# MLP stage written out: signals, split engines, gate and add apart

## The chip, the cores and the metric

One core of one Trainium2 chip runs the program. The metric is the device time of one execution in microseconds (us). The kernel before took 4002.65 us, the median of three runs (3992.6 to 4006.91).

TensorE (PE) multiplies, VectorE (DVE), ScalarE (ACT) and GpSimd (POOL) work on elements, and SyncE (SP) issues the DMAs of the stage in question. Each works through its own queue in order and waits for others by semaphores.

## The reference

Two transformer blocks on x of 2 x 2048 x 512, in float32: a cross attention, then self attention, cross attention and an MLP. The change is in the MLP alone:

```python
h = layer_norm(x)
h = h * (1.0 + scale_mlp) + shift_mlp
h = jax.nn.gelu(h @ mlp_w1 + mlp_b1) @ mlp_w2 + mlp_b2
x = x + h * gate_mlp
return x
```

w1 is 512 x 2048, w2 is 2048 x 512. The modulated layer norm is written by the stage before, transposed, as `u`.

## The kernel before

`build` calls the stages one after the other; `mlp` is the last. Every float32 matrix is held as two parts of type float32r, an upper one (rounded) and a lower one (the rest), and a product is three matmuls (`PARTS`): upper by upper, upper by lower, lower by upper.

The 4096 tokens are worked through in eight chunks of 512 (W), numbered n = 2i + b: `Fori` loops on every engine run i over four steps, with b = 0 and 1 written out in the body. The hidden dimension of 2048 is 16 tiles m of 128.

PE: `hidden(m)` makes 12 matmuls from w1 and `us` into PSUM tile `ph` (L2220); `output(m)` makes 12 from `gs` and w2 into the four row tiles of `py` (L2235), which collect over m. The order is hidden 0, hidden 1, output 0, hidden 2, output 1 and so on to output 15, then hidden 0 of the next chunk.

ScalarE: GELU with bias b1 from `ph` into `gelu` (L2262). VectorE: the split of `gelu` into the upper part by a cast (L2277) and the lower by a subtraction (L2279), both into `gs`. `gelu` and `gs` have two buffers each. After output 15 VectorE gates `py` (L2283, into `gated`) and adds to `x` (L2285), four row tiles in turn, and only then comes to the splits of the next chunk. GpSimd adds the gated bias row to x as soon as x has been loaded (L2300).

The weights come in eight pieces of 1 MB, w1 and w2 in turn; hidden tiles 0 to 3 need piece 0, output tiles 0 to 3 piece 1, hidden 4 to 7 piece 2 and so on. Pieces 0 and 1 are rounded by ScalarE (L2253, L2255) and subtracted by VectorE (L2269); both first wait for `small_in`, that is b1 and four rows, or, VectorE, for ScalarE. Pieces 2 to 7 are split by GpSimd (L2291, L2293), after which it multiplies the bias row by the gate (L2295).

SP's order is: piece 0, both parts of `us` for chunk 0, piece 1, b1 (L2166), rows (L2168, L2169), pieces 2 to 7; then for each chunk the load of x (after the store of the chunk before), the load of `us` for the next chunk, and the store of x (L2189).

Of the kernel before, what the change touches and what calls it, by code (L numbers as in the profile page):

```python
# [7 lines left out]
F32 = mybir.dt.float32  # L8
# [5 lines left out]
P = 128  # L14
# [6 lines left out]
W = 512  # L21
# [16 lines left out]
def column(ap):  # L38

    return ap.rearrange("(t p) -> p t", p=P)  # L40
# [12 lines left out]
def chunk_after(i, b):  # L53
    return (i, 1) if b == 0 else (i + 1, 0)
# [2067 lines left out]
def mlp(nc, d, u_in, x_in, gate, out):  # L2122


    with nc.cleanup_on_exit(), ExitStack() as ctx:
# [12 lines left out]
        gated = sb("gated", [P, 2, W])  # L2138
# [4 lines left out]
        small_in = sem("small_in")  # L2143
        w_hi, w_lo, rows_done = sem("w_hi"), sem("w_lo"), sem("rows_done")
        late_hi, late_lo = sem("late_hi"), sem("late_lo")
# [3 lines left out]
        passed = sem("passed")  # L2149
# [8 lines left out]
        SMALL = 1 + 2 * B  # L2158

        @block.sync  # L2160
        def _(sp):
            sp.sem_inc(stored, DMA)

            def load_small():
                with nc.allow_non_contiguous_dma(reason="a short vector, once"):
                    sp.dma_start(b1[:], column(d["L1_xcond_mlp_b1"])).then_inc(small_in, DMA)  # L2166
# [4 lines left out]
            def load_u(i, b, first=False):  # L2171
                if not first:

                    sp.wait_ge(used, (2 * i + b - 1) * HT + 2)
                    sp.sem_inc(passed, 1)
                for part in range(2):
                    sp.dma_start(us[:, b, part].bitcast(F32), u_in[part, b, :, bass.ds(i * W, W)].rearrange("(t p) w -> p t w", p=P)).then_inc(u_loaded[b], DMA)  # L2177

            def chunk(i, b, left):
                sp.wait_ge(stored, DMA * (2 * i + b + 1))  # L2180


                sp.sem_inc(passed, 1)
                sp.dma_start(x[:], x_in[b, bass.ds(i * W, W), :].rearrange("(t p) c -> p t c", p=P)).then_inc(x_loaded, DMA)
                if left > 1:
                    load_u(*chunk_after(i, b))
                sp.wait_ge(x_ready, (2 * i + b + 1) * TT)
                sp.sem_inc(passed, 1)
                sp.dma_start(out[b, bass.ds(i * W, W), :].rearrange("(t p) c -> p t c", p=P), x[:]).then_inc(stored, DMA)  # L2189

            def load_weights(k):
                sp.dma_start(pieces[k][2], pieces[k][3]).then_inc(raw_in[k], DMA)  # L2192

            load_weights(0)
# [5 lines left out]
            with sp.Fori(0, CHUNKS - 1) as i:  # L2200
                for b in range(B):
                    chunk(i, b, 3)
            for b in range(B):
                chunk(CHUNKS - 1, b, B - b)
            sp.wait_ge(stored, DMA * (B * CHUNKS + 1))

        @block.tensor
        def _(pe):
            def hidden(i, b, m):
                n = 2 * i + b  # L2210
                if m == 0:
                    pe.wait_ge(w_lo, 1)
                elif m % KT == 0:
                    pe.wait_ge(late_lo, 2 * (m // KT) - 1)
                if m == 0:
                    pe.wait_ge(u_loaded[b], 2 * DMA * (i + 1))
                pe.wait_ge(gelu_done, n * HT + m + 1)
                for t in range(KT):
                    for s, (pm, pw) in enumerate(PARTS):
                        mm = pe.matmul(ph[:, m % 4], w1[pw][:, t, m * P:(m + 1) * P], us[:, b, pm, t],  # L2220
                                       start=(t == 0 and s == 0), stop=(t == KT - 1 and s == 2))
                mm.then_inc(hidden_done, 1)

            def output(i, b, m):
                n = 2 * i + b
                if m == 0:
                    pe.wait_ge(w_lo, 2)
                elif m % KT == 0:
                    pe.wait_ge(late_lo, 2 * (m // KT))
                if m == 0:  # L2230
                    pe.wait_ge(y_read, n * TT + 1)
# [7 lines left out]
            pe.sem_inc(used, 2)  # L2239
            with pe.Fori(0, CHUNKS) as i:  # L2240
                for b in range(B):
                    for m in range(HT + 1):
                        if m < HT:
                            hidden(i, b, m)
                        if m > 0:
                            output(i, b, m - 1)

        @block.scalar
        def _(act):
            act.sem_inc(gelu_done, 4)  # L2250
            act.wait_ge(small_in, DMA * SMALL)
            act.wait_ge(raw_in[0], DMA)
            act.activation(pieces[0][0], pieces[0][2], ACT.Copy).then_inc(w_hi, 1)  # L2253
            act.wait_ge(raw_in[1], DMA)
            act.activation(pieces[1][0], pieces[1][2], ACT.Copy).then_inc(w_hi, 1)  # L2255
            with act.Fori(0, CHUNKS) as i:
                for b in range(B):
                    n = 2 * i + b
                    for m in range(HT):
                        act.wait_ge(used, n * HT + m + 1)  # L2260
                        act.wait_ge(hidden_done, n * HT + m + 1)
                        act.activation(gelu[:, m % 2], ph[:, m % 4], ACT.Gelu_apprx_tanh, bias=b1[:, m:m + 1]).then_inc(gelu_done, 1)  # L2262

        @block.vector
        def _(dve):
            dve.sem_inc(y_read, 1)
            for k, (hi, lo, raw, _) in enumerate(pieces[:2]):
                dve.wait_ge(w_hi, k + 1)
                dve.tensor_tensor(lo, raw, hi.bitcast(F32), ALU.subtract).then_inc(w_lo, 1)  # L2269
            dve.wait_ge(small_in, DMA * SMALL)  # L2270
            with dve.Fori(0, CHUNKS) as i:
                for b in range(B):
                    n = 2 * i + b
                    for m in range(HT):
                        dve.wait_ge(gelu_done, n * HT + m + 5)
                        dve.wait_ge(used, n * HT + m + 1)
                        dve.tensor_copy(gs[:, m % 2, 0], gelu[:, m % 2]).then_inc(g_hi, 1)  # L2277
                        dve.wait_ge(g_hi, n * HT + m + 1)
                        dve.tensor_tensor(gs[:, m % 2, 1], gelu[:, m % 2], gs[:, m % 2, 0].bitcast(F32), ALU.subtract).then_inc(g_lo, 1)  # L2279
                    dve.wait_ge(used, (n + 1) * HT + 2)  # L2280
                    dve.wait_ge(biased, n + 1)
                    for tt in range(TT):
                        dve.tensor_tensor(gated[:, tt % 2], py[:, tt], grow[:, b], ALU.mult).then_inc(y_read, 1)  # L2283
                        dve.wait_ge(y_read, n * TT + tt + 2)
                        dve.tensor_tensor(x[:, tt], x[:, tt], gated[:, tt % 2], ALU.add).then_inc(x_ready, 1)  # L2285

        @block.gpsimd
        def _(pool):
            for k, (hi, lo, raw, _) in enumerate(pieces[2:]):
                pool.wait_ge(raw_in[2 + k], DMA)  # L2290
                pool.tensor_copy(hi, raw).then_inc(late_hi, 1)  # L2291
                pool.wait_ge(late_hi, k + 1)
                pool.tensor_tensor(lo, raw, hi.bitcast(F32), ALU.subtract).then_inc(late_lo, 1)  # L2293
            pool.wait_ge(small_in, DMA * SMALL)
            pool.tensor_tensor(brow[:], brow[:], grow[:], ALU.mult).then_inc(rows_done, 1)  # L2295
            pool.wait_ge(rows_done, 1)
            with pool.Fori(0, CHUNKS) as i:
                for b in range(B):
                    pool.wait_ge(x_loaded, DMA * (2 * i + b + 1))
                    pool.tensor_tensor(x[:], x[:], brow[:, b].unsqueeze(1).to_broadcast([P, TT, C]), ALU.add).then_inc(biased, 1)  # L2300
# [58 lines left out]
```

## Time and profile before

| what | value |
|---|---|
| median of three runs | 4002.65 us |
| profiled execution | 4006.39 us |
| its span | 4004.6 us |
| mean granted clock of PE | 0.938 |
| PE matmuls busy | 3667.1 us (92%) |
| VectorE, ScalarE, GpSimd busy | 2261.2, 1862.3, 2175.1 us |
| MLP stage in the span | 3248.20 to 4004.6 us |

The profile's times are microseconds from the start of the span. [...] "Idle before" is what an engine waited ahead of an instruction, with the one that released it. Time behind SPq is that of issuing a DMA, and landing is counted from the issue.

### The profile page before, as it was taken

Reading aid. Unit: us, or ns where it says so; the run is one execution under the profiler, and the core shown is the slowest. Engines: PE = TensorE matmul, PEld = TensorE weight load, DVE = VectorE, ACT = ScalarE, POOL = GpSimd, SP = SyncE. Lnnn points to the kernel's source line nnn. Section 1 sums busy time; section 2 is a strip of 40 time slices with the busy share of each in tenths; the row PEclk is TensorE's granted clock in tenths of the full one; section 3 lists DMA queues with packets and bytes.
Section 4 is the critical chain, followed back from the end, with each engine's and each line's share of the span. In section 5 each row is a group of like instructions: output and inputs, shape, how many; then the busy total and the mean of one; then the engine's idle time right before and its main releaser. Section 6 shows DMA issues by size and latency. Waiting matters only on the chain. (4 is left out here: it accounts for less than half of the span.)

```text
span 4004.6 us, 50633 instructions
## 1 busy us (share of the span) xinstructions
PE 3667.1 (92%) x18828; PEld 2414.8 (60%) x18828; DVE 2261.2 (56%) x3958; ACT 1862.3 (47%) x3439; POOL 2175.1 (54%) x1075
## 2 busy tenths in 40 slices
PE   4799969979999999999999999958999959999998
PEld 2577748855555445454545455427777737888887
DVE  2466642228777777777777777515665634222222
ACT  1465651113666666666666666644665521111111
POOL 0356630004888888888888888864777542000000
PEclk8798889987999999999999999978999879999999
DMA  7566556764464645556464644444576551111110
GB/s 230 146 160 168 166 159 218 222 185 105 98 143 103 149 108 127 124 110 137 101 145 106 153 101 111 120 123 111 153 179 172 134 200 42 42 42 42 42 42 31
DMA packets 231940, 505.60 MB, mean 126 GB/s; under 512 B 38151, under 2 KB 55047, under 8 KB 211751
## 3 DMA queue, kind: packets, MB, share of 16 engines
q1 hardware_dynamic: 213287, 368.49, 33.6%
q0 software_dynamic: 18432, 134.23, 15.4%
q8 instruction: 131, 2.15, 0.2%
q14 instruction: 90, 0.74, 0.1%
HBM read 215.54 MB, written 144.51 MB: 90 GB/s over the span
## 5 line engine op out<-in xcount | busy, mean ns | idle before, releaser
L2003 DVE TENSOR_REDUCE a_peak<-a_sm 128x1 f32<-128x512 f32 x2048 | 1263.3, 680 | 396.0 <-PE a_sm L1822 394.7
L1959 ACT ACTIVATE a_e<-a_st 128x512 f32<-128x512 f32 x2048 | 1061.6, 604 | 539.1 <-PE a_st L1844 506.5
L2070 POOL TENSOR_TENSOR a_esum<-a_esum,a_e 128x2048 f32<-128x2048 f32 x256 | 1210.2, 4727 | 18.8 <-POOL a_esum L2070 0.4
L1822 PE MATMUL a_sm<-a_k,a_q 96*128 96x512 f32 x2048 | 883.9, 439 | 27.9 <-DMA a_k<-s_k 27.9
L1844 PE MATMUL a_st<-a_q,a_k 128*128 128x512 f32 x2048 | 827.2, 406 | 17.4 <-ACT a_e L1959 17.2
L1822 PEld LDWEIGHTS a_sm<-a_k,a_q 96*128 96x128 f32 x2048 | 394.8, 193 | 475.8 <-DVE a_peak L2003 337.5
L1857 PE MATMUL a_acc<-a_e,a_v 128*32 128x512 f32 x4096 | 505.7, 600 | 0.0
L1844 PEld LDWEIGHTS a_st<-a_q,a_k 128*128 128x128 f32 x2048 | 387.9, 190 | 137.3 <-ACT a_e L1959 62.8
L2220 PE MATMUL mlp_ph<-mlp_us,mlp_w_hi 128*128 128x512 f32 x1024 | 336.4, 391 | 33.0 <-DVE mlp_raw_lo L2269 33.0
L2262 ACT ACTIVATE mlp_gelu<-mlp_ph,mlp_b 128x512 f32<-128x512 f32 x128 | 88.1, 688 | 595.1 <-PE mlp_ph L2220 595.1
L2277 DVE CAST mlp_gs<-mlp_gelu 128x512 fp32r<-128x512 f32 x128 | 90.8, 709 | 459.0 <-ACT mlp_gelu L2262 459.0
L2300 POOL TENSOR_TENSOR mlp_x<-mlp_x,mlp_brow 128x2048 f32<-128x2048 f32 x8 | 36.9, 4616 | 569.7 <-DMA mlp_x<-s_x 569.4
L2235 PE MATMUL mlp_py<-mlp_w_hi,mlp_gs 128*128 128x512 f32 x1024 | 317.6, 391 | 16.9 <-DVE mlp_gs L2279 16.9
L1433 POOL TENSOR_TENSOR p_e<-p_e,p_inv 128x308 f32<-128x308 f32 x256 | 173.2, 708 | 175.5 <-DVE p_inv L1109 175.4
L2220 PEld LDWEIGHTS mlp_ph<-mlp_us,mlp_w_hi 128*128 128x128 f32 x1024 | 193.5, 189 | 73.7 <-issue 33.4
L1857 PEld LDWEIGHTS a_acc<-a_e,a_v 128*32 128x32 f32 x4096 | 100.4, 108 | 219.6 <-ACT a_e L1959 124.7
L2235 PEld LDWEIGHTS mlp_py<-mlp_w_hi,mlp_gs 128*128 128x128 f32 x1024 | 191.8, 188 | 61.3 <-issue 16.3
L589 PE MATMUL p_sm<-p_ks,p_qs 96*128 96x78 f32 x1024 | 171.5, 310 | 51.0 <-DMA p_qs<-s_q 30.1
L589 PEld LDWEIGHTS p_sm<-p_ks,p_qs 96*128 96x128 f32 x1024 | 157.1, 222 | 82.8 <-DMA p_qs<-s_q 28.3
L2220 PE MATMUL mlp_ph<-mlp_us,mlp_raw_lo 128*128 128x512 f32 x512 | 200.1, 391 | 0.0
L2235 PE MATMUL mlp_py<-mlp_raw_lo,mlp_gs 128*128 128x512 f32 x512 | 199.9, 390 | 0.0
L1094 DVE TENSOR_REDUCE p_top<-p_sm 128x4 f32<-128x308 f32 x256 | 118.4, 465 | 142.5 <-PE p_sm L589 140.5
(155 smaller groups left out, 5255.1 us busy)
## 6 DMA issues: line engine op xcount, KB each, us to landing
a_esum_moved<-a_e POOLq DMA_DIRECT2D x128, 1024.0 KB, 7.3
p_qs<-s_q SPq DMA_DIRECT2D x192, 256.0 KB, 5.7
s_q<-p_qo SPq DMA_DIRECT2D x64, 512.0 KB, 7.2
a_q<-s_q SPq DMA_DIRECT2D x96, 256.0 KB, 6.8
a_k<-s_k SPq DMA_DIRECT2D x24, 1024.0 KB, 15.7
s_x<-p_x SPq DMA_DIRECT2D x16, 1024.0 KB, 4.4
s_u<-p_ut_hi SPq DMA_DIRECT2D x64, 256.0 KB, 5.8
s_u<-p_ut_lo SPq DMA_DIRECT2D x64, 256.0 KB, 6.3
```

What stands on the lines that cost most here:

```text
L589: mm = pe.matmul(sm[:, unit % 2, h * KE:(h + 1) * KE], qs[0:3 * DH, g % 2, h, qt * P:(qt + 1) * P], ks[0:3 * DH, b, g * GH + h], start=Tru ...
L1094: dve.tensor_reduce(top[:, unit % 4], src, AX.X, ALU.max).then_inc(top_done, 1)
L1433: pool.tensor_tensor(e[:, number % 2, qt, :, 0:S], e[:, number % 2, qt, :, 0:S], inv[:, number % 2, qt].unsqueeze(2).to_broadcast([P, GH, ...
L1822: mm = pe.matmul(sm[:, bank_of_unit(j, u), x * KE:(x + 1) * KE], q[0:3 * DH, j % QR, h, qt * P:(qt + 1) * P], k[0:3 * DH, g % 2, h, kc * K ...
L1844: pe.matmul(st[0:KR, place(kt, h) % RING], k[:, g % 2, h, kt * P:kt * P + KR], q[:, j % QR, h], start=True, stop=True).then_inc(score_done, 1)
L1857: mm = pe.matmul(acc[rows, 0], v[0:KR, g % 2, kt, rows], e[0:KR, (j * NKT + kt) % ER, h], start=(kt == 0), stop=(kt == NKT - 1), tile_posi ...
L1959: act.activation(e[0:KR, (j * NKT + kt) % ER, h], st[0:KR, place(kt, h) % RING], ACT.Exp, scale=SCALE).then_inc(score_read, 1)
L2003: dve.tensor_reduce(dst, src, AX.X, ALU.max).then_inc(unit_read, 1)
L2070: pool.tensor_tensor(esum[:], e[:, slot(0)] if x == 1 else esum[:], e[:, slot(x)], ALU.add).then_inc(e_added, 1)
L2220: mm = pe.matmul(ph[:, m % 4], w1[pw][:, t, m * P:(m + 1) * P], us[:, b, pm, t], start=(t == 0 and s == 0), stop=(t == KT - 1 and s == 2))
L2235: mm = pe.matmul(py[:, tt], gs[:, m % 2, pw, tt * P:(tt + 1) * P], w2[pm][:, m], start=(m == 0 and s == 0), stop=(m == HT - 1 and s == 2))
L2277: dve.tensor_copy(gs[:, m % 2, 0], gelu[:, m % 2]).then_inc(g_hi, 1)
```

## The change

The loops are gone: all engines run over n = 0 to 7 in straight code, and the semaphore counts start at zero, with the early waits left out instead of counted up in advance.

Loads: b1 has a signal of its own (`b1_in`) and is issued behind `us` and ahead of piece 1; the four rows are issued behind all weights, then `us` of chunk 1. Within a later chunk SP's order is load of x, load of the next `us`, store of x; the store waits for adds that now come in the next chunk. The last chunk is stored in four row tiles.

ScalarE loads the table for GELU ahead of all, waits for piece 0 without the small vectors, rounds pieces 0 and 1, and rounds 2 to 7 behind the GELUs of tiles 0, 1, 4, 5, 8 and 9 of chunk 0. VectorE subtracts behind the splits of the same tiles. GpSimd has the bias row and x left.

VectorE gates the four row tiles at the end of a chunk (into four buffers instead of two) and adds them to x behind the splits of tiles 0 to 3 of the next chunk; in the last chunk gate and add stay together. PE waits for each row tile of `py` by itself.

```diff
-        gated = sb("gated", [P, 2, W])
+        gated = sb("gated", [P, TT, W])
...
+        SMALL = 2 * B
+        N = B * CHUNKS
+        place = lambda n: (n // B, n % B)
+        BEHIND = {0: 2, 1: 3, 4: 4, 5: 5, 8: 6, 9: 7}
...
+            def load_u(n):
+                i, b = place(n)
+                if n >= 2:
+                    sp.wait_ge(used, (n - 1) * HT)
...
+            def load_x(n):
+                i, b = place(n)
+                if n:
+                    sp.wait_ge(stored, DMA * n)
...
+            def store_x(n):
+                i, b = place(n)
+                sp.wait_ge(x_ready, (n + 1) * TT)
...
+            def store_row(n, tt):
+                i, b = place(n)
+                sp.wait_ge(x_ready, n * TT + tt + 1)
+                sp.dma_start(out[b, i * W + tt * P:i * W + (tt + 1) * P, :], x[:, tt]).then_inc(stored, DMA)
...
             load_weights(0)
-            load_u(0, 0, True)
-            load_weights(1)
-            load_small()
-            for k in range(2, NP):
+            load_u(0)
+            with nc.allow_non_contiguous_dma(reason="a short vector, once"):
+                sp.dma_start(b1[:], column(d["L1_xcond_mlp_b1"])).then_inc(b1_in, DMA)
+            for k in range(1, NP):
                 load_weights(k)
...
+            load_rows()
+            load_u(1)
+            for n in range(N):
+                load_x(n)
+                if n and n + 1 < N:
+                    load_u(n + 1)
+                if n < N - 1:
+                    store_x(n)
+            for tt in range(TT):
+                store_row(N - 1, tt)
...
+            def output(n, m):
+                if m % KT == 0:
+                    pe.wait_ge(w_lo, 2 * (m // KT) + 2)
                 pe.wait_ge(g_lo, n * HT + m + 1)
                 for tt in range(TT):
+                    if m == 0 and n:
+                        pe.wait_ge(y_read, (n - 1) * TT + tt + 1)
...
+            act.preload_act_table_set("gelu_apprx_tanh_and_others")
+            round_weights(0)
+            round_weights(1)
+            act.wait_ge(b1_in, DMA)
+            for n in range(N):
+                for m in range(HT):
+                    act.wait_ge(hidden_done, n * HT + m + 1)
+                    if n * HT + m >= 2:
+                        act.wait_ge(g_lo, n * HT + m - 1)
+                    act.activation(gelu[:, m % 2], ph[:, m % 4], ACT.Gelu_apprx_tanh, bias=b1[:, m:m + 1]).then_inc(gelu_done, 1)
+                    if n == 0 and m in BEHIND:
+                        round_weights(BEHIND[m])
...
+            weights_rest(0)
+            weights_rest(1)
+            for n in range(N):
+                for m in range(HT):
+                    split(n, m)
+                    if n == 0 and m in BEHIND:
+                        weights_rest(BEHIND[m])
+                    if n and m < TT:
+                        add_output(n - 1, m)
+                if n == 0:
+                    dve.wait_ge(small_in, DMA * SMALL)
+                for tt in range(TT):
+                    gate_output(n, tt)
+                    if n == N - 1:
+                        add_output(n, tt)
...
-            for k, (hi, lo, raw, _) in enumerate(pieces[2:]):
-                pool.wait_ge(raw_in[2 + k], DMA)
-                pool.tensor_copy(hi, raw).then_inc(late_hi, 1)
-                pool.wait_ge(late_hi, k + 1)
-                pool.tensor_tensor(lo, raw, hi.bitcast(F32), ALU.subtract).then_inc(late_lo, 1)
```

## Rows read from the trace of the kernel before

**Rows 1.** Page: busy us of the engines, share of the span, instructions.

```profile
PE 3667.1 (92%) x18828; PEld 2414.8 (60%) x18828; DVE 2261.2 (56%) x3958; ACT 1862.3 (47%) x3439; POOL 2175.1 (54%) x1075
```

**Rows 2.** Windows, one chunk each: busy us (count) by engine, PE's clock, DMA share, GB/s.

```profile
3273.05:3373.99 100.94, 92.51 (x384) 74.55 (x385) 56.43 (x33) 12.29 (x17) 50.05 (x14) 0.96 0.19 71
3373.99:3462.55 88.56, 87.35 (x386) 72.04 (x385) 24.67 (x40) 11.01 (x16) 4.60 (x1) 1.00 0.14 48
3462.55:3551.07 88.52, 87.26 (x386) 71.95 (x385) 24.59 (x40) 12.29 (x17) 4.60 (x1) 1.00 0.13 47
```

**Rows 3.** Chain of waits, first chunk: start us, us, what.

```profile
3273.05 5.31 PE mlp_ph L2220 x12
...
3283.87 4.58 PE mlp_py L2235 x12
...
3291.19 2.72 PE mlp_py L2235 x12
```

**Rows 4.** Timeline of the head: start us, us, engine, instruction [idle before <-releaser]; then chain.

```profile
3268.57 1.91 ACT L2253 ACTIVATE mlp_w_hi<-mlp_raw 128x2048 fp32r<-128x2048 f32 x1 [27.04 <-DMA mlp_grow<-s_gates]
3273.05 0.79 PE L2220 MATMUL mlp_ph<-mlp_us,mlp_w_hi 128*128 128x512 f32 x1 [33.01 <-DVE mlp_raw_lo L2269]
...
3270.51 2.30 DVE mlp_raw_lo L2269
```

**Rows 5.** SP's issues; landings of piece 0, of both `us` parts, of piece 1.

```profile
3249.73 0.82 SPq L2192 DMA_DIRECT2D mlp_raw<-in_L_xcond_mlp_w  x1
3252.80 8.87 SPq L2168 DMA_DIRECT2D mlp_brow<-in_L_xcond_mlp_b  x1
...
DMA to landing us min/median/max: 5.6/5.6/5.6
DMA to landing us min/median/max: 7.9/9.0/10.0
DMA to landing us min/median/max: 12.4/12.4/12.4
```

**Rows 6.** Window of the first tile (columns as in rows 2); PE's waits, 3284 to 3373.

```profile
3273.00:3277.60 4.60, 4.54 (x11) 3.58 (x12) 3.70 (x1) 0.00 (x0) 4.52 (x2) 0.50 1.05 388
...
PE mlp_py L2235 <- DVE mlp_gs L2279: 8.4, 5, 2.8
```

**Rows 7.** DMA, 3260 to 3262.5, packets; then a window of 2 us.

```profile
DMA packets 2227, 0.31 MB, mean 124 GB/s; under 512 B 2080, under 2 KB 2080, under 8 KB 2227
...
3260.00:3262.00 2.00, 0.00 (x0) 0.00 (x0) 0.00 (x0) 0.00 (x0) 0.00 (x0) 0.50 0.94 139
```

**Rows 8.** Timeline: casts beside GpSimd in chunks 0 and 1, and a subtraction undisturbed.

```profile
3297.33 4.93 POOL L2293 TENSOR_TENSOR mlp_raw_lo<-mlp_raw,mlp_w_hi 128x2048 fp32r<-128x2048 f32 x1
3297.72 4.82 DVE L2277 CAST mlp_gs<-mlp_gelu 128x512 fp32r<-128x512 f32 x1
...
3331.91 0.69 DVE L2279 TENSOR_TENSOR mlp_gs<-mlp_gelu,mlp_gs 128x512 fp32r<-128x512 f32 x1
...
3392.85 2.11 DVE L2277 CAST mlp_gs<-mlp_gelu 128x512 fp32r<-128x512 f32 x1 [4.29 <-ACT mlp_gelu L2262]
```

**Rows 9.** Timeline of the first boundary, chunk 0 to chunk 1.

```profile
3374.19 0.69 DVE L2283 TENSOR_TENSOR mlp_gated<-mlp_py,mlp_grow 128x512 f32<-128x512 f32 x1 [3.50 <-PE mlp_py L2235]
3376.97 0.69 ACT L2262 ACTIVATE mlp_gelu<-mlp_ph,mlp_b 128x512 f32<-128x512 f32 x1 [7.47 <-PE mlp_ph L2220]
3379.51 0.42 DVE L2277 CAST mlp_gs<-mlp_gelu 128x512 fp32r<-128x512 f32 x1
3380.80 0.70 PE L2235 MATMUL mlp_py<-mlp_w_hi,mlp_gs 128*128 128x512 f32 x2 [1.21 <-DVE mlp_gs L2279]
```

**Rows 10.** DMA issues: count, KB each, median us to landing, of the two stages.

```profile
out<-mlp_x SPq DMA_DIRECT2D x7, 1024.0 KB, 4.3
...
s_u<-p_ut_lo SPq DMA_DIRECT2D x2, 256.0 KB, 3.2
```

**Rows 11.** DMA queue 8, 3325 to 3462: packets, MB, share of 16 engines.

```profile
q8 instruction: 5, 0.08, 0.2%
```

More of the change, by code:

```diff
@@ L2157, in mlp, with load_rows @@
         raw_in = [sem(f"raw_in{k}") for k in range(NP)]
-        SMALL = 1 + 2 * B
+        SMALL = 2 * B
+        N = B * CHUNKS
+        place = lambda n: (n // B, n % B)
+        BEHIND = {0: 2, 1: 3, 4: 4, 5: 5, 8: 6, 9: 7}
         @block.sync
         def _(sp):
[L2162 to L2166, printed above, removed]
+            def load_rows():
                 for b in range(B):
@@ L2179, in chunk @@
[L2179 to L2189, printed above, removed]
+                    sp.dma_start(us[:, n % 2, part].bitcast(F32), u_in[part, b, :, i * W:(i + 1) * W].rearrange("(t p) w -> p t w", p=P)).then_inc(u_loaded[n % 2], DMA)
@@ L2207, in _, with hidden @@
+            for tt in range(TT):
+                store_row(N - 1, tt)
+            sp.wait_ge(stored, DMA * (N - 1 + TT))
         @block.tensor
         def _(pe):
-            def hidden(i, b, m):
-                n = 2 * i + b
+            def hidden(n, m):
+                if m % KT == 0:
+                    pe.wait_ge(w_lo, 2 * (m // KT) + 1)
                 if m == 0:
[L2212 to L2217, printed above, removed]
+                    pe.wait_ge(u_loaded[n % 2], 2 * DMA * (n // 2 + 1))
+                if n * HT + m >= 4:
+                    pe.wait_ge(gelu_done, n * HT + m - 3)
@@ L2237, in output @@
                 mm.then_inc(used, 1)
[L2239 to L2246, printed above, removed]
+            for n in range(N):
+                for m in range(HT + 1):
+                    if m < HT:
+                        hidden(n, m)
+                    if m > 0:
+                        output(n, m - 1)
@@ L2248, in _, with round_weights @@
         @block.scalar
         def _(act):
[L2250 to L2262, printed above, removed]
+            def round_weights(k):
+                act.wait_ge(raw_in[k], DMA)
+                act.activation(pieces[k][0], pieces[k][2], ACT.Copy).then_inc(w_hi, 1)
@@ L2264, in _, with weights_rest @@
         @block.vector
         def _(dve):
-            dve.sem_inc(y_read, 1)
-            for k, (hi, lo, raw, _) in enumerate(pieces[:2]):
+            def weights_rest(k):
+                hi, lo, raw, _ = pieces[k]
                 dve.wait_ge(w_hi, k + 1)
                 dve.tensor_tensor(lo, raw, hi.bitcast(F32), ALU.subtract).then_inc(w_lo, 1)
[L2270 to L2285, printed above, removed]
@@ new lines, in split, with gate_output @@
+            def split(n, m):
+                dve.wait_ge(gelu_done, n * HT + m + 1)
+                if n * HT + m >= 2:
+                    dve.wait_ge(used, n * HT + m - 1)
+                dve.tensor_copy(gs[:, m % 2, 0], gelu[:, m % 2]).then_inc(g_hi, 1)
+                dve.wait_ge(g_hi, n * HT + m + 1)
+                dve.tensor_tensor(gs[:, m % 2, 1], gelu[:, m % 2], gs[:, m % 2, 0].bitcast(F32), ALU.subtract).then_inc(g_lo, 1)
+            def gate_output(n, tt):
+                if tt == 0:
+                    dve.wait_ge(used, (n + 1) * HT)
+                if n:
+                    dve.wait_ge(x_ready, (n - 1) * TT + tt + 1)
+                dve.tensor_tensor(gated[:, tt], py[:, tt], grow[:, place(n)[1]], ALU.mult).then_inc(y_read, 1)
@@ new lines, in add_output @@
+            def add_output(n, tt):
+                dve.wait_ge(biased, n + 1)
+                dve.wait_ge(y_read, n * TT + tt + 1)
+                dve.tensor_tensor(x[:, tt], x[:, tt], gated[:, tt], ALU.add).then_inc(x_ready, 1)
+            weights_rest(0)
+            weights_rest(1)
+            for n in range(N):
+                for m in range(HT):
[10 more added lines that the diff above has]
+                        add_output(n, tt)
@@ L2296, in _ @@
             pool.wait_ge(rows_done, 1)
[L2297 to L2300, printed above, removed]
+            for n in range(N):
+                pool.wait_ge(x_loaded, DMA * (n + 1))
+                pool.tensor_tensor(x[:], x[:], brow[:, place(n)[1]].unsqueeze(1).to_broadcast([P, TT, C]), ALU.add).then_inc(biased, 1)
 def build(nc, d, out):
```

28 lines of the change are left out of this document (5 added, 23 removed).

## The prediction

> **What bounds the kernel now.** I read the page first: TensorE (PE) is busy for 92% of the span, and the chain of waits inside the MLP stage runs tile after tile through its two matmul lines, L2220 and L2235 [rows 1, 3]. The diff touches only that stage, from the first load at 3248.20 to the end at 4004.6, about 756 of 4004.6 us, so I then read the stage chunk by chunk [rows 2]. A chunk is 32 tiles of 12 matmuls. Where PE is not disturbed a tile takes 2.72 us [rows 3], so a chunk needs 32 x 2.72 = 87.04 us and eight need 696.3. The stage lasts 756.4. The other 60 us are in four places, and they are all that the change can touch: the head (3248.20 to 3273.05, 24.85 us), the first chunk (100.94, so 13.9 too many), the seven later chunks (about 88.5, so 1.5 too many each, 10.4 in all) and the tail after the last matmul (10.8).
>
> **The head.** PE's first matmul waited for the lower part of the first weights (VectorE), that for ScalarE's rounding, and ScalarE stood at L2251 for the five small vectors until 3268.57 [rows 4]. Its real inputs had long been there: piece 0 landed 5.6 us after its issue, at 3253.8, and the slower half of `us` 10.0 us after its issue at about 3249.17, at 3259.15 [rows 5]. ScalarE now waits for piece 0 alone. Its rounding takes 1.94 to the hand-over and VectorE's subtraction 2.30 more [rows 4], so the weights are ready by 3253.9 + 4.3 = 3258.2, before `us` at 3259.15. PE therefore starts at 3259.3, the landing plus the usual 0.15: **13.75 us** earlier. Next late is `us`, and the table load (12.29 less 11.01 us of ScalarE, the difference of a chunk with one and a chunk without [rows 2]: 1.28) now lies in the empty time before.
>
> **The first chunk.** PE runs hidden 0 in 5.31 us and hidden 1 in about 2.75 [rows 3, 4], to 3267.4. The granted clock is 0.50 over the first 4.6 us after its long idle time and full after that [rows 6]; I keep that, since the idle time ahead is still over 10 us. Then output 0 needs piece 1, and here is a new wait. L2255 was done in one go behind L2253 before; now ScalarE waits for piece 1 with the first GELU queued behind it, VectorE with the first split queued behind its subtraction, and PE for that split. Piece 1 landed at 3249.73 + 12.4 = 3262.1 [rows 5], but b1 now goes ahead of it on SP's queue. b1 is 2048 tiny packets: over 3260.0 to 3262.5 the DMA engines move 2080 packets under 512 bytes and 0.31 MB, where they otherwise move 388 GB/s, so about 2.0 us are lost [rows 6, 7]. The bounds are 1.3 us of delay (the stretch from 3260 to 3262 at 139 instead of 388 GB/s) and 8.9, the time that SP stood on the issue right behind b1 [rows 5, 7]; nearer to the first I take 2.0, because most of the 8.9 was spent behind 4 MB of big transfers that were still in the queue. Piece 1 then lands at 3264.1, and 0.15 + 1.9 rounding + 2.3 subtraction + 1.3 split (0.42 and 0.69 with hand-overs [rows 8, 9]) put output 0 at 3269.8. PE idles 2.4 us, about as before (2.8), and I let output 0 take 4.58 us again, as after that idle time before [rows 3]; without the slowing it would be 1.9 less. The other 29 tiles take 78.9. That gives the end of chunk 0 at 3269.8 + 4.6 + 78.9 = 3353.3, if nothing else stalls.
>
> What stalled it before: GpSimd's six casts and six subtractions of weights (4.93 for one of the latter) ran beside VectorE's; a cast that needs 0.42 alone took 4.82, from beside the start of GpSimd's subtraction to its end, and PE waited 8.4 us in five places of this chunk, 2.8 of them the wait for output 0 [rows 6, 8]. These splits move to ScalarE (1.9 each) and VectorE (2.3 each). Per step of 5.44 us ScalarE then has 0.69 + 1.9 and VectorE 1.1 + 2.3 = 3.4, which PE's two tiles hide; piece 2 lands 2.7 us behind piece 1, in time for the ScalarE slot behind the first GELU, and each later one is due 10 us or more after it is in. Were one of them to run right ahead of a split, its 2.3 would still fit: a split is ready 3.2 us before PE wants it. What GpSimd still does in this chunk is the row product and the addition to x (4.60 [rows 2]); with x behind all other loads, landing near 3294, the latter starts about when VectorE casts for tile 5. I book one stall of 1.0 for it, the size of those of before (1.2). Chunk 0 ends at 3354.3 instead of 3373.99, **19.7 us** earlier, head included.
>
> **Seven boundaries.** Before, VectorE did gate and add four times (5.32 us from 3374.19 on, 1.33 a pair) before its first split of the next chunk: the cast began at 3379.51, though the GELU had been ready since 3377.7, and PE waited 1.21 us for it at 3380.80 [rows 9]. A chunk without it takes 87.04, so each boundary costs 1.49 with the slower first matmuls. Now only four gates (0.68 each [rows 9]) stand ahead: from 3374.19 they end at 3376.9 on that time scale, the GELU at 3377.7 is last, its split is ready at 3378.9 and PE wants it at 3379.4. The adds (0.69) go behind splits 0 to 3, where VectorE waited 4.29 us in a step [rows 8]. py is freed gate by gate, all before output 0 needs it. The store of x moves about 13 us later and the next x load, its addition and the load of `us` with it; they were due 60 us later, so nothing waits. At the even chunks the table load that stood before the first GELU (1.28) goes too; it would otherwise now be late by some 0.6. Seven times 1.49: **10.4 us**. Lower bound: 0.5 left of each, 7; nothing can go below the 87.04.
>
> **The tail.** Gates and adds keep their 5.4 us. The last store is now one row tile (256 KB) instead of 1 MB. The 1 MB store took 4.3 us to land, a 256 KB store 3.2 in the stage before, between the same memories [rows 10]: **1.1 us**, between 0 and (an estimate from the two rows, with the part that goes by bytes gone wholly) 2.0. The three stores ahead of it leave 1.33 apart and are gone.
>
> **Unrolling.** The loops over two chunks become straight code. PE runs ahead of its loop's return: a chunk that begins with a loop's return takes 88.52, one that begins within the body 88.56 [rows 2]. So nothing is gained. The other way: straight code must be fetched. During the first pass over the body, 3325 to 3462, five instruction packets came in on queue 8 [rows 11] and PE was waiting for nothing but VectorE, so I book nothing. [...]
>
> **Sum.** 19.7 + 10.4 + 1.1 = 31.2 us. The profiled execution took 4006.39 us (span 4004.6), so its like would take 3975.2. The median of the three timed runs is 3.7 lower at 4002.65, and I forecast 4002.65 - 31.2 = 3971. These runs spread over 14 us, and 0.3% (12 us) is about what a measurement of this kernel can tell from no change.
>
> **Rivals.**
> 1. *The new wait on piece 1 is the long one.* If b1 really costs the 8.9 us, piece 1 lands at 3271.0, output 0 starts at 3276.7 and 6.9 of the gain go: 3978. For it speaks the row of 8.9 us, against it the 4 MB in front of that issue. Chance 0.10.
> 2. *GpSimd's addition to x meets a cast in every chunk.* It moves to about 29.6 us after a chunk's start, and the casts for tiles 5 and 6 come at 28.3 and 33.7. If it starts 1.5 to 2.8 us sooner, or 2.6 later, the cast is held up to 4.6 us with 3.2 to spare: at most 1.4 lost in each of six chunks, 8 us: 3979. Before, a cast so met took 2.11 us and ended with GpSimd's instruction [rows 8], and PE did not notice. [...] Chance 0.08.
> 3. *Slower: PE starves on its own code.* The MLP's PE code grows from one body of two chunks to four; at five or six packets a body that is some 22 to 24 fetches instead of 6. The 31.2 us are eaten at 1.3 us a fetch, and at 1.9 us each the kernel is slower by 12 us: 4015. Against it: none of the five fetches in the first pass shows as idle time of PE. Chance 0.03.
> 4. *No difference: the change does not do what it says.* With the first weights' signal alone the head is gone, but the splits behind the activations stall PE by some 1.2 us in three steps as before, and the boundaries keep their bubble, since ScalarE's GELU and not VectorE ends last: of the sum 13.75 less those 3.7 stay, 10 us: 3993. Against it stands the GELU's end at 3377.7, 1.8 us before the cast began [rows 9]. Chance 0.04.
> The forecast has 0.75.
>
> **Range.** The low end adds output 0 at full clock (1.9), no stall (1.0), the best tail (0.9) and some 7 us of the run-to-run spread: 3961. The high end holds rivals 1 and 2 and some 4 of spread: 3983. Faster by over 0.3%: 0.93 (forecast and rivals 1 and 2); within: 0.04 (rival 4); slower: 0.03 (rival 3).
>
> **What would show it.** PE's first MLP matmul some 11 us after the stage's first issue instead of 24.9; PE's one wait before L2235's first matmul 2 to 3 us; no wait of PE at the other boundaries and chunks of 87.0 us; casts of 0.43 throughout but for the one or two beside GpSimd; ScalarE with one table load; the last store landing within 3.3 us. I am wrong if a chunk past the first stays above 87.5, if the first matmul comes after 3262 on the old time scale, or if PE shows idle time that no engine released.

## The result and the profile after

The changed kernel takes 3960.93 us, the median of six runs (3955.17 to 3965.67); the kernel before, run beside it as well, 3996.11 (six runs, 3992.6 to 4006.91). The ratio is 0.9908, 95% interval 0.9892 to 0.9924, a fall of 35.2 us between the medians. The forecast was a fall of 31.2 us and a time of 3971, with a range from 3961 to 3983: the direction and the mechanism held, and the time lies 0.07 us below the range.

The page of the changed kernel, first its busy times, which answer to [rows 1], and the queue of the instruction fetches:

```profile
span 3957.4 us, 50108 instructions
...
PE 3653.0 (92%) x18828; PEld 2407.2 (61%) x18828; DVE 2229.0 (56%) x3964; ACT 1869.1 (47%) x3442; POOL 2133.2 (54%) x1063
...
q8 instruction: 149, 2.44, 0.3%
```

VectorE and GpSimd are busy 32 and 42 us less, ScalarE 7 more: that is work that moved, or that no longer runs beside the other's (a cast of 0.42 us took 4.82 beside GpSimd's subtraction [rows 8]). But the span is 47.2 us shorter than that of before, more than the medians differ. So the MLP stage has to be measured by itself, from SP's first issue to the end. That issue is at 3235.06 in this execution and was at 3248.20 in that of before; the stage takes 722.34 instead of 756.40 us, **34.06 us** less. The other 13.1 us lie ahead of it, in code that the change doesn't touch (more on them below).

The windows of the first four chunks of the changed kernel (us, busy by engine, PE's clock, DMA share, GB/s), as [rows 2]:

```profile
3246.07:3339.39 93.32, 90.82 (x385) 74.50 (x386) 38.80 (x39) 23.77 (x23) 7.00 (x2) 0.96 0.34 124
3339.39:3426.43 87.04, 87.04 (x385) 72.07 (x385) 22.83 (x40) 11.04 (x16) 4.94 (x1) 1.00 0.14 49
3426.43:3513.47 87.04, 87.04 (x385) 72.07 (x385) 22.83 (x40) 11.04 (x16) 4.81 (x1) 1.00 0.13 49
3513.47:3600.51 87.04, 87.04 (x385) 72.07 (x385) 22.83 (x40) 11.04 (x16) 4.83 (x1) 1.00 0.14 49
```

From the second chunk on PE is busy in the whole of each window, at the floor of 32 x 2.72 us. The waits of PE in the stage have shrunk to two, and both are in the head:

```profile
PE mlp_ph L2223 <- DMA mlp_us<-s_u: 19.2, 1, 19.2
PE mlp_py L2235 <- DVE mlp_gs L2278: 2.5, 1, 2.5
```

The timeline of the head shows the new order, one line for each of its steps (compare [rows 4, 5]):

```profile
3235.06 0.39 SPq L2176 DMA_DIRECT2D mlp_raw<-in_L_xcond_mlp_w  x1
3235.07 1.28 ACT L2252 ACT_TABLE_LOAD   x1 [6.75 <-PEq L336]
...
3246.07 0.76 PE L2223 MATMUL mlp_ph<-mlp_us,mlp_w_hi 128*128 128x512 f32 x1 [19.24 <-DMA mlp_us<-s_u]
...
3250.47 1.92 ACT L2250 ACTIVATE mlp_w_hi<-mlp_raw 128x2048 fp32r<-128x2048 f32 x1 [8.39 <-DMA mlp_raw<-in_L_xcond_mlp_w]
...
3252.43 2.29 DVE L2270 TENSOR_TENSOR mlp_raw_lo<-mlp_raw,mlp_w_hi 128x2048 fp32r<-128x2048 f32 x1 [8.02 <-ACT mlp_w_hi L2250]
...
3255.93 0.81 PE L2235 MATMUL mlp_py<-mlp_w_hi,mlp_gs 128*128 128x512 f32 x2 [2.50 <-DVE mlp_gs L2278]
```

PE starts 11.0 us after the first issue and then waits for piece 1, which ScalarE gets 15.4 us after it; rounding, subtraction and split follow one another, and output 0 starts at 20.9. It takes 4.58 us at a mean granted clock of 0.63, as it did before.

At a boundary (here the first) two of the four gates are one row, the GELU follows, and the split is 0.8 us ahead of PE, which needs it at 3344.83:

```profile
3340.70 1.28 DVE L2285 TENSOR_TENSOR mlp_gated<-mlp_py,mlp_grow 128x512 f32<-128x512 f32 x2
3342.15 0.69 ACT L2261 ACTIVATE mlp_gelu<-mlp_ph,mlp_b 128x512 f32<-128x512 f32 x1 [7.47 <-PE mlp_ph L2223]
3342.87 0.43 DVE L2276 CAST mlp_gs<-mlp_gelu 128x512 fp32r<-128x512 f32 x1 [0.89 <-ACT mlp_gelu L2261]
3343.33 0.69 DVE L2278 TENSOR_TENSOR mlp_gs<-mlp_gelu,mlp_gs 128x512 fp32r<-128x512 f32 x1
3343.94 0.68 DVE L2290 TENSOR_TENSOR mlp_x<-mlp_x,mlp_gated 128x512 f32<-128x512 f32 x1
```

The last row there is the first add, now behind the split. From the end of the last matmul to the end of the span it is 8.7 us instead of 10.8.

### The profile page after: what moved, and what is told of

The parts are those of the page before. It is cut to its first block and busy times, and to the rows that moved or that the text cites. A ratio compares the mean times of both kernels' runs of the same rounds, so it can differ in the third digit from the quotient of the medians.

```text
span 3957.4 us, 50108 instructions
## 1 busy us (share of the span) xinstructions
PE 3653.0 (92%) x18828; PEld 2407.2 (61%) x18828; DVE 2229.0 (56%) x3964; ACT 1869.1 (47%) x3442; POOL 2133.2 (54%) x1063
## 5 line engine op out<-in xcount | busy, mean ns | idle before, releaser
L2276 DVE CAST mlp_gs<-mlp_gelu 128x512 fp32r<-128x512 f32 x128 | 58.1, 454 | 462.7 <-ACT mlp_gelu L2261 462.7
L2223 PEld LDWEIGHTS mlp_ph<-mlp_us,mlp_w_hi 128*128 128x128 f32 x1024 | 192.9, 188 | 59.8 <-issue 19.6
```

## Experiments

Times of the whole kernel can't tell 2 us. So each run below is read by its stage, from the stage's first issue to the end of the span, in one execution, where before is 756.40 and the changed kernel 722.34. A second execution of the changed kernel gave 722.11 us, but that agreement is partly luck: output 0 took 3.00 us in it instead of 4.58, and a stall in chunk 0, which the first doesn't have, cost 1.1. A difference of stages below some 1.6 us therefore counts only where the rows show where it comes from.

### Only written out

```diff
-            with pe.Fori(0, CHUNKS) as i:
+            for i in range(CHUNKS):
```

(in the kernel before, and likewise on the other four engines).

> The kernel before with the MLP's loops written out and nothing else changed. My reading (straight code costs nothing and gains nothing): the MLP stage, first issue to end of span, stays at 756.4 us, within 1, with some 18 more instruction packets on queue 8 and no idle time of PE that no engine released. Rival (a loop's return costs a fetch, so that unrolling itself is part of the gain): the chunks that began with a return get shorter and the stage loses several us. Rival (straight code starves PE): stage 780 us or more.

Stage 755.72 us, instruction packets 149 on queue 8 instead of 131, and PE's waits the same twelve for L2279 (16.7 us against 16.9). The timed ratio to the kernel before is 1.0009 (0.9999 to 1.0018). Writing out is neither a gain nor a loss that these runs can tell. It takes three of the four table loads away by itself, and the bubbles at the boundaries stay at 1.2 us of waiting, so they don't come from the table loads or the loop. The 0.7 us lie ahead of the first matmul (24.12 after the first issue against 24.85); whether they belong to the loop's set-up or to the loads of one execution stays open.

### Only the head

```diff
             load_u(0, 0, True)
-            load_weights(1)
-            load_small()
-            for k in range(2, NP):
+            with nc.allow_non_contiguous_dma(reason="a short vector, once"):
+                sp.dma_start(b1[:], column(d["L1_xcond_mlp_b1"])).then_inc(b1_in, DMA)
+            for k in range(1, NP):
                 load_weights(k)
+            load_small()
...
-            act.wait_ge(small_in, DMA * SMALL)
             act.wait_ge(raw_in[0], DMA)
```

> The kernel before, loops kept, with only the signals of the head changed: b1 has its own, stands behind us and ahead of piece 1, the rows are issued behind the weights, and ScalarE waits for piece 0 alone. My reading: PE's first matmul 11.0 us after the stage's first issue instead of 24.85, output 0 after about 21 instead of 35.7, all later stalls as before, so the stage takes 756.4 - 14.5 = 742 us. Rival (the head hands its gain on to the splits: GpSimd is late for tiles that PE now wants 14 us sooner): the first chunk from its first matmul to the next chunk's gets 5 us or more longer than 100.9 and the stage takes 747 or more.

Stage 749.87 us: only **6.5** of the 14.5 us arrive. PE's first matmul is 11.25 us after the first issue, but output 0 now waits 8.1 us. PE's waits in the stage, and VectorE's and GpSimd's rows ahead of output 0:

```profile
PE mlp_py L2234 <- DVE mlp_gs L2277: 21.9, 11, 8.1
...
3255.46 3.27 POOL L2290 CAST mlp_w_hi<-mlp_raw 128x2048 fp32r<-128x2048 f32 x1 [23.85 <-DMA mlp_raw<-in_L_xcond_mlp_w]
3256.89 2.12 DVE L2275 CAST mlp_gs<-mlp_gelu 128x512 fp32r<-128x512 f32 x1
3258.81 4.55 POOL L2292 TENSOR_TENSOR mlp_raw_lo<-mlp_raw,mlp_w_hi 128x2048 fp32r<-128x2048 f32 x1
3259.04 4.86 DVE L2277 TENSOR_TENSOR mlp_gs<-mlp_gelu,mlp_gs 128x512 fp32r<-128x512 f32 x1
```

With the rows out of the way piece 2 lands right behind piece 1, so that GpSimd begins just as VectorE comes to its first split: the cast ends with GpSimd's cast (2.12 instead of 0.43), and the subtraction of 0.69 takes 4.86, to the end of GpSimd's. My reading of 742 was wrong. The rival's two numbers came true (747 or more for the stage, and the first chunk 7.1 us longer than 100.9), but it put the loss at later tiles, and most of it is at output 0.

### GpSimd's splits put back

```diff
-        BEHIND = {0: 2, 1: 3, 4: 4, 5: 5, 8: 6, 9: 7}
+        BEHIND = {}
...
+            for k, (hi, lo, raw, _) in enumerate(pieces[2:]):
+                pool.wait_ge(raw_in[2 + k], DMA)
+                pool.tensor_copy(hi, raw).then_inc(late_hi, 1)
+                pool.wait_ge(late_hi, k + 1)
+                pool.tensor_tensor(lo, raw, hi.bitcast(F32), ALU.subtract).then_inc(late_lo, 1)
```

> The changed kernel with pieces 2 to 7 split by GpSimd again, all in one go as they land. My reading: VectorE's casts beside GpSimd take up to 4.8 us again and PE stalls 1.2 us in four or five steps of the first chunk; the stage takes 722.3 + 6 = 728 us. Rival (the stalls came from the late start and not from the splits): the stage stays at 722.3, within 1.

Stage 737.58 us, **15.2** more than the changed kernel where I had 6. That is too much for my reading and against the rival. PE's waits before output tiles, and the same pair of instructions as above:

```profile
PE mlp_py L2240 <- DVE mlp_gs L2283: 14.9, 5, 8.2
...
3259.76 4.55 POOL L2319 TENSOR_TENSOR mlp_raw_lo<-mlp_raw,mlp_w_hi 128x2048 fp32r<-128x2048 f32 x1
3259.99 4.87 DVE L2283 TENSOR_TENSOR mlp_gs<-mlp_gelu,mlp_gs 128x512 fp32r<-128x512 f32 x1
```

Output 0 starts 6.4 us later than in the changed kernel (27.3 after the first issue against 20.9), the same collision as in the run with the head alone; the other 8.8 us are PE's four later waits (6.7) and the tiles slowed behind all five.

### Only the splits

```diff
+            act.wait_ge(b1_in, DMA)
+            act.wait_ge(small_in, DMA * SMALL)
             round_weights(0)
             round_weights(1)
-            act.wait_ge(b1_in, DMA)
```

(with the old order of loads, and gate and add in pairs).

> The changed kernel with the old head (b1 and rows ahead of pieces 2 to 7, ScalarE waiting for all small vectors before it rounds) and gate and add in pairs: against the kernel before, only the splits have moved, the loops are straight and the last store is by rows. The run with GpSimd's splits was 15.2 us longer than the changed kernel, where I had booked 6 to 7. If the extra 8 us come only where the head is early as well (GpSimd meets the splits ahead of output 0), this kernel takes 756.4 - 2.1 (tail) - 6.7 (stalls) = 747.6 us in the stage. Rival (the move is worth 15.2 wherever it stands): 739.

Stage 745.36 us, between my 747.6 and the rival's 739, and nearer to mine. Less the tail (2.1) and what the straight code showed (0.7), the splits alone are worth **8.2** us. Head (6.53) and splits (8.24) alone make 14.8; together, in the run of the next section, which keeps the pairs, they are worth 756.40 - 733.97 - 2.1 - 0.7 = 19.6. So 4 to 5 us of the gain exist only if both are done, because the early head brings GpSimd's splits into the way of output 0. (The finer figure isn't to be had from single executions, in which output 0 alone takes 3.0 or 4.6 us.)

### Gate and add in pairs again

```diff
-                    if n and m < TT:
-                        add_output(n - 1, m)
...
                     gate_output(n, tt)
-                    if n == N - 1:
-                        add_output(n, tt)
+                    add_output(n, tt)
```

> The changed kernel with gate and add of a row tile together at the end of each chunk, as before. My reading: every one of the seven later chunks gets its bubble back, 1.49 us each, so they take 88.5 us and the stage 722.3 + 10.4 = 732.7. Rival (the bubble went because ScalarE's table load and the loop are gone): chunks of 87.0 to 87.3 and a stage below 725.

Stage 733.97 us, 11.6 more where I had 10.4. PE's waits:

```profile
PE mlp_py L2235 <- issue: 10.2, 7, 1.5
PE mlp_py L2235 <- DVE mlp_gs L2278: 2.8, 2, 2.0
```

The seven bubbles are back, without a table load and without a loop: the later chunks take 88.76 us each, 1.72 over the floor, 12.0 in all. That is more than the 1.5 each of before, since a pair of gate and add takes 1.40 us here instead of 1.33. The profile puts the waits down to issue; VectorE's rows show its split right behind the last pair. Chunk 0 is 0.5 us shorter than in the changed kernel: output 0 took 2.98 instead of 4.58, but in this execution GpSimd's addition to x came ahead of a subtraction, which took 4.99 us, and PE waited 0.8 us for it. That is the stall of 1.0 that I had booked. The second profile of the changed kernel has both as well (two waits, 2.8 us, the longest 1.9). In its first profile the addition held up the cast of the same tile instead (3.62 us), which ended in time for PE.

### One store at the end

```diff
-                if n < N - 1:
-                    store_x(n)
-            for tt in range(TT):
-                store_row(N - 1, tt)
+                store_x(n)
```

> The changed kernel with the last chunk stored in one piece of 1 MB. My reading: only the tail changes, from 8.7 us after the last matmul back to 10.8, stage 722.3 + 2.1 = 724.4 us. Rival (the tail is set by gate and add, and the 2.1 came with something else): stage within 0.5 of 722.3.

Stage 724.74 us; the time behind the last matmul is 10.9 again instead of 8.7, which is 2.2 of the 2.4. The four stores by rows landed 2.0 us after their issue each:

```profile
L2192 SPq DMA_DIRECT2D out<-mlp_x x4: 332/342/350, 3950.2 to 3954.4; - x4
...
DMA to landing us min/median/max: 2.0/2.0/2.0
```

### b1 behind piece 1, and b1 three times

```diff
+            load_weights(1)
             with nc.allow_non_contiguous_dma(reason="a short vector, once"):
                 sp.dma_start(b1[:], column(d["L1_xcond_mlp_b1"])).then_inc(b1_in, DMA)
-            for k in range(1, NP):
+            for k in range(2, NP):
                 load_weights(k)
```

> The changed kernel with b1 issued behind piece 1 instead of ahead of it. My reading (output 0 hangs on piece 1's landing, which b1 holds up by some 2 us): piece 1 lands and output 0 starts 1.9 us sooner; PE's wait ahead of it shrinks from 2.5 to about 0.6, and if the granted clock then doesn't fall, output 0 takes 2.7 instead of 4.6: stage 720.4, or 718.6 with that. Rival (b1 is now what the first GELU waits for): no change or a gain below 0.5.

```diff
                 sp.dma_start(b1[:], column(d["L1_xcond_mlp_b1"])).then_inc(b1_in, DMA)
+                for y in range(2):
+                    sp.dma_start(spare[:, y], column(d["L1_xcond_mlp_b1"])).then_inc(spare_in, DMA)
```

> The changed kernel with b1's load issued three times in a row ahead of piece 1, two of them into spare room: the price of one such load by doubling it. My reading: 1.6 to 2 us for each of the two, output 0 3.2 to 4 us later, stage 725.5 to 726.4. Rival (8.9 us each, as the issue behind b1 took before): output 0 some 18 us later, stage 740.

Stage 719.30 and 726.24 us. ScalarE rounds piece 1 1.4 us sooner without b1 ahead of it (14.0 after the first issue) and 3.24 later with two more (18.65): **1.4 to 1.6 us** for one load of 2048 packets of four bytes, not 8.9. (In the six other executions with one b1 ahead of piece 1 the rounding began at 15.4 to 16.0, so single executions give the price only to some 0.6.) The rest of both differences is output 0's own time, which goes with PE's clock: 4.58, 3.00 and 5.25 us at a mean granted clock of 0.63, 1.00 and 0.54. The rows of output 0 from the three chains go with waits of 2.5, 0.3 and 5.2 us ahead of it:

```profile
3255.93 4.58 PE mlp_py L2235 x12
...
3258.44 3.00 PE mlp_py L2236 x12
...
3258.55 5.25 PE mlp_py L2240 x12
```

(the first of the changed kernel, the second of the run with b1 late, the third of the one with b1 three times). With the wait down to 0.3 the tile is 1.6 us shorter than in the first profile of the changed kernel, which is why moving b1 by one place gives 3.0 against it and not 1.4. But the tile can be that short with b1 ahead too. In the second profile it took 3.00 behind a wait of 1.95:

```profile
3256.54 3.00 PE mlp_py L2235 x12
```

Against that execution the run with b1 late gains 2.8: 1.6 in the start of output 0 and 1.1 in the stall, which it doesn't have.

### Matmuls on zeros ahead of hidden 0

```diff
+            pe.wait_ge(warm_set, 1)
+            for y in range(WARM):
+                pe.matmul(py[:, y % TT], gs[:, 0, 0, 0:P], gs[:, 0, 0], start=True, stop=True)
```

> The changed kernel with 24 extra matmuls on zeros on PE, ahead of hidden 0 while it waits for the loads. My reading: hidden 0 and 1 run at the full clock and end 2.6 us sooner, but output 0 waits for piece 1 all the same, so the wait grows by as much and the stage stays at 722.3, within 0.5. Rival (the low clock of the first tile is on the path): the stage gets 2 to 4 us shorter.

(24 of them, `WARM = 24`.) Stage 722.82 us, no gain: output 0 still starts when piece 1 is ready. But the run doesn't test what I meant it to. The matmuls on zeros end at 3246.40, PE then waits 2.6 us for `us`, and hidden 0 and 1 take 7.3 us as without them:

```profile
3249.01:3256.30 7.29, 7.29 (x24) 5.54 (x24) 0.74 (x1) 2.49 (x2) 0.00 (x0) 0.77 0.97 336
```

The mean clock over the two tiles is 0.77, and 0.76 in the changed kernel. That the low clock of these two tiles is off the path stays argued: PE waits 2.7 us for piece 1 behind them.

### Pieces cut, and the two together

```diff
-        BEHIND = {0: 2, 1: 3, 4: 4, 5: 5, 8: 6, 9: 7}
+        BEHIND = {0: 2, 1: 3, 2: 4, 3: 5, 6: 6, 7: 7, 10: 8, 11: 9}
+        NEED_1, NEED_2 = {0: 1, 2: 3, 4: 5, 8: 7, 12: 9}, {0: 2, 1: 4, 4: 6, 8: 8, 12: 10}
...
+            parts = [(0, 2), (0, 1), (2, 4), (1, 4)] if k == 0 else [] if k == 1 else [(c * KT, (c + 1) * KT)]
```

(the first w1 piece as 256 and 256 columns, the first w2 piece as tile 0 and tiles 1 to 3; b1 stands behind the first part of each, ahead of the second).

> The changed kernel with the first two pieces cut: columns 0 to 255 of w1, us, tile 0 of w2, b1, the rest of w1's first piece, the rest of w2's; each part rounded and subtracted by itself. My reading: PE's first matmul at 9.6 us after the first issue (0.5 MB less ahead of it), no wait ahead of output 0 (17.7), which then takes 2.7 us: stage 722.3 - 5.1 = 717.2. Rival (the smaller transfers and more signals cost what they save): 720 or more.

> As the run with cut pieces, and 28 matmuls on zeros on PE ahead of hidden 0 so that the granted clock is full when it begins. My reading: hidden 0 and 1 take 5.4 us instead of 8.1, and since output 0 no longer waits for piece 1, this now counts: stage 714.6, 0.9889 of the kernel before, 7 to 8 us under the changed kernel. Rival (as in the run with extra matmuls alone: output 0 waits all the same): the stage of the run with cut pieces.

Stage 716.58 us with the pieces cut and 715.57 with the extra matmuls as well, 5.8 and 6.8 under the changed kernel. Chain of waits of the run with cut pieces:

```profile
3246.11 7.87 DMA mlp_us<-s_u
3253.98 0.14 issue
3254.11 7.09 PE mlp_ph L2231 x24
3261.21 2.72 PE mlp_py L2243 x12
```

PE starts 9.0 us after the first issue, hidden 1 is followed by output 0 without a wait, and output 0 takes 2.72 us at a granted clock of 1.00; the stage is 0.6 under my 717.2. With 28 matmuls on zeros, which reach up to hidden 0 without a gap, the first two tiles take 5.59 us at a mean granted clock of 1.00 instead of 7.09 at 0.79. I had expected 8.1 without them, so there were only 1.5 us to be had instead of 2.7; hidden 0 starts 0.3 later in this execution, where `us` landed later by as much, and output 1 takes 2.92, which leaves 1.0. The 7 to 8 us that I expected under the changed kernel were 6.8. Timed on one chip (four and five runs), the changed kernel is at 0.9907 (0.9892 to 0.9923) of the kernel before and the one with both at 0.9903 (0.9886 to 0.9919), medians 3960.99 and 3960.31: the 6.8 us that the stage shows don't appear in the timed runs. That gain is shown for the stage alone.

### The changed kernel again

No edit; the runs are those behind the first of the two ratios just given.

> The changed kernel again, as it is, on the same chip as the two below. My reading: stage 722.3 us within 1, and the rest of what its runs differ by lies in the stages before it, which this change doesn't touch. Against the kernel before: 0.991, 34 us. Rival (the change also moves earlier stages, by 13 us in the profiled pair): a difference of 40 us or more.

The stage was 722.11 us. This comparison has a fall of 39.7 us between the medians (4000.67 before), the first one 35.2, with almost the same ratio (0.9907 and 0.9908). 39.7 is nearer to the rival's 40 than to my 34, so the medians don't refute it. The profiles speak against it: in the runs with the head alone and with the loops alone, which keep the rest of the kernel before, the MLP begins at 3236.93 and 3241.58, within the 3234.46 to 3245.24 of the changed kernel and its variants.

## Why the prediction was right and where it was wrong

**By its own steps**, in us after the stage's first issue or as a gain:

| step | predicted | profiled pair |
|---|---|---|
| hidden 0 starts | 11.1 | 11.0 |
| output 0 starts | 21.6 | 20.9 |
| chunk 0 ends | 106.1 | 104.3 |
| gain to there | 19.7 | 21.5 |
| seven boundaries | 10.4 | 10.5 |
| tail | 1.1 | 2.1 |
| sum | 31.2 | 34.1 |

**What held.** The waits named for the head were those that ended last: `us` for hidden 0, piece 1 for output 0, with the GELU and the split queued behind it. The later chunks fell to 87.04 each, and the run with pairs shows by what. The straight code cost nothing (a timed ratio of 1.0009 with the loops only written out). ScalarE's and VectorE's splits are hidden by PE's tiles (PE's one wait behind hidden 0 is the 2.5 us ahead of output 0). Rival 1 (a long wait on piece 1), rival 3 (PE starving on its code) and rival 4 (no difference) are out. Rival 2 was near: GpSimd's addition to x starts 28.6 us after a chunk's start (3368.02), 1.0 sooner than forecast, where the rival needed 1.5. It starts 0.2 us behind the subtraction for tile 5 and ends at 3372.96, 0.17 us into the next cast, which takes 0.46 instead of 0.43:

```profile
3367.81 0.69 DVE L2278 TENSOR_TENSOR mlp_gs<-mlp_gelu,mlp_gs 128x512 fp32r<-128x512 f32 x1
3372.79 0.46 DVE L2276 CAST mlp_gs<-mlp_gelu 128x512 fp32r<-128x512 f32 x1 [4.29 <-ACT mlp_gelu L2261]
```

These rows and those of the run with the head alone show both orders. VectorE's subtraction that starts 0.2 us ahead keeps its 0.69 us, and GpSimd's instruction gets longer, 4.94 instead of the 4.60 of before; where GpSimd starts 0.2 us ahead (3258.81), its subtraction takes 4.55 and VectorE's 0.69 become 4.86.

**The step that failed: what the fall was taken from.** I subtracted from 4002.65, the median of three runs, of which two turned out to be the longest of the six in the comparison above, whose median is 3996.11. Twenty-nine timed runs of the kernel before lie between 3987.22 and 4007.18, with their median at 3996.75. (The nine of the second comparison alone have 4000.67, so a median still hangs on which runs are taken.) So the base was 5.9 to 6.5 us too high, out of the 10.1 us by which the forecast was; the rest is the fall, 35.2 by the medians instead of 31.2, less 0.4 of rounding. With the base at 3996.11 the same sum gives 3964.9, and with the base as it was the 34.1 us of the profiled pair would have given 3968.6, inside the range. I had seen a spread of 14 us in three runs, but allowed 7 us of it at the low end and 4 at the high one and kept the centre on the three. The low end itself comes to 3960.65 by its own terms, which I rounded up to 3961. That the time lies 0.07 us under it is chance, since the six runs spread over 10.5 us; that it lies 10 us from the centre is not.

One profile of the kernel before couldn't show that its own execution was a long one: its MLP begins at 3248.20, and in the thirteen other profiled executions, all with the same code ahead of it, at 3234.46 to 3245.24. For the profiled pair 12.5 of the 13.1 us lie in the stage ahead of the MLP: SP issues its load of `p_grow` there at 2657.95 in the one and at 2657.28 in the other. (In other executions that issue comes up to 7.5 us later than in that of before, so the stages ahead of it scatter too.) Windows from 2650 to the MLP's first issue, of before, of the changed kernel and of the run with b1 three times:

```profile
2650.00:3248.20 598.20, 503.88 (x2688) 397.82 (x2688) 331.12 (x662) 303.10 (x555) 352.80 (x318) 0.86 0.57 148
...
2650.00:3235.06 585.06, 495.88 (x2688) 390.96 (x2688) 327.22 (x662) 302.53 (x554) 353.88 (x318) 0.87 0.58 151
...
2650.00:3234.46 584.46, 493.74 (x2696) 387.52 (x2696) 328.23 (x662) 303.64 (x555) 354.09 (x319) 0.88 0.58 151
```

PE does the same matmuls in 8 and 10 us less, at a mean granted clock of 0.87 and 0.88 instead of 0.86; the other 5 us of the pair's difference are time in which PE is idle. So the difference ahead of the stage goes with the clock granted there, and whether the clock or the idle time comes first isn't shown. That straight code in the MLP doesn't bring it, the timed ratio of the run with the loops only written out shows (1.0009). What decides the clock's course from execution to execution is open.

**Terms of the sum that were mis-sized**, 2.9 us together, all to the same side. The tail: 1.1 instead of 2.1, because I took the landing of a 256 KB store from a stage with other transfers beside it (3.2 us); alone it is 2.0. The stall in chunk 0: booked at 1.0, it comes in some executions and not in the profiled one. b1: 2.0 for what is 1.4 to 1.6, most of the 0.7 at output 0; my own row gave 1.7 (2.5 us at 124 instead of 388 GB/s), not 2.0. The rest, 0.2, are the loads and the boundaries. The 4.58 us that I let output 0 take came in this execution and not in the second, where it took 3.00: there the stage agrees by luck. In rival 3 I set all 22 to 24 fetches against the gain, though only some 18 were new (149 packets instead of 131); none showed as idle time.

**Right for the pair, but not for each part.** The table of steps hides that I had credited the head with 13.75 us by itself and the splits with the 5.6 us of stalls that the trace of before shows. Alone they give 6.5 and 8.2. The trace of before showed the collision at output 0 only in part. There GpSimd had piece 2 at 3271.29, 9.3 us ahead of VectorE's first split, and its subtraction was nearly over when that came:

```profile
3274.64 6.51 POOL L2293 TENSOR_TENSOR mlp_raw_lo<-mlp_raw,mlp_w_hi 128x2048 fp32r<-128x2048 f32 x1
3280.56 0.87 DVE L2277 CAST mlp_gs<-mlp_gelu 128x512 fp32r<-128x512 f32 x1 [3.85 <-ACT mlp_gelu L2262]
3281.47 2.26 DVE L2279 TENSOR_TENSOR mlp_gs<-mlp_gelu,mlp_gs 128x512 fp32r<-128x512 f32 x1
```

With the early head the same GpSimd instruction begins 0.2 us ahead of VectorE's subtraction, which then takes 4.86. That had to be worked out from what the earlier head moves. I did so for GpSimd's addition to x, but not for the kernel in which one part is missing.

## What to carry to other kernels

A step that frees a transfer also moves the engine that waits for it (with the early head alone GpSimd began its splits 18.5 instead of 23.1 us after the stage's first issue): before you credit an earlier start with its whole length, lay the new landing times beside what the engines of the critical path do then. Here it was VectorE's subtraction of 0.69 us, which took 4.86 beside GpSimd's. Work behind a critical instruction instead of ahead of it can take a stall away completely (with the adds behind the next splits the later chunks took 87.04 us, in pairs 88.76), and cost nothing here, where VectorE still waited 3.69 us in a step behind an add. And where a stage can be read to 1 or 2 us but the kernel only to 10, give the change from the stage, and take the base from as many runs as there are, with its spread at both ends.

## What the runs showed of the hardware that I had not expected

- A short wait of PE can cost more than itself. Output 0, the same twelve matmuls in each of these runs, took 3.00 us after a wait of 0.3, 3.00 and 2.98 after 1.95 and 1.98, 4.52 after 2.13, 4.58 after 2.50, 4.46 after 2.72 and 5.25 after 5.2; elsewhere, without a wait, such a tile takes 2.72. The mean granted clock over the tile was 1.00 in the first three, 0.62 to 0.63 in the next three and 0.54 in the last. Inside output 0 of the changed kernel it is 0.50 in the windows from 3256.50 to 3259.00 and 1.00 from 3260.00 on. These are single executions, all in the head of the stage, and where a wait begins to cost the clock they don't settle; but two executions of one kernel fall on either side.
- One load of 2048 elements of four bytes costs the queue behind it 1.4 to 1.6 us of transfers, though SP stands for 7.9 us at the next issue behind it (3237.42 to 3245.36 in the changed kernel), in which the DMA engines move 369 GB/s.
- GpSimd's subtraction stretched VectorE's subtraction as much as its casts (0.69 to 4.86 us, against 0.42 to 4.82 for a cast). In the trace of before the same subtractions (L2279) had taken 2.74 at most.
